# Four edits to a transformer block on one core: order of early work, row staging, statistics, slot products

## The chip, the cores and the metric

The kernel runs on one core of a Trainium2 chip. A core has five engines that run their own instruction queues and meet only at semaphores: PE (matmul), DVE (vector), ACT (scalar activations), POOL (GpSimd) and SP (here: issuing DMAs). The metric is the device time of one execution in microseconds, the median of 3 runs.

## What is computed

Two layers of cross-attention, each followed by a routed feed-forward, on x of 4 batches x 512 tokens x 256, with a context of 4 x 1024 x 256:

```python
def _L0_xattn_ref(encoder_hc, decoder_hq, w_sim, b_sim, W_qv, b_qv):
    Sim = (encoder_hc @ w1)[:, :, None] + (decoder_hq @ w2)[:, None, :] + jnp.einsum('bid,bjd->bij', encoder_hc * w3, decoder_hq) + b_sim[0]
    A = jax.nn.softmax(Sim, axis=2)
    hq_hat = jnp.einsum('bij,bjd->bid', A, decoder_hq)
    Batt = jax.nn.softmax(jnp.max(Sim, axis=2), axis=1)
    hc_bar = jnp.einsum('bi,bid->bd', Batt, encoder_hc)[:, None, :]
    feats = jnp.concatenate([encoder_hc, hq_hat, encoder_hc * hq_hat, encoder_hc * hc_hat], axis=-1)
    return feats @ W_qv + b_qv
...
x = x + _L0_xattn_ref(_layernorm(x, axis=-1), ctx_1024, ...)
x = x + _L0_ffn_ref(_layernorm(x, axis=-1), ...)     # top 2 of 12, 8 experts of 512 (silu), 4 pass x through
x = x + _L1_xattn_ref(_layernorm(x, axis=-1), ctx_1024, mask, ...)   # 4 heads of 64
x = x + _L1_ffn_ref(_layernorm(x, axis=-1), ...)     # top 2 of 8 experts of 1024 (gelu)
return x
```

## The kernel before

Tokens lie in 16 tiles of 128 rows, four to a batch; x stays in SBUF (`m.x`). Products that need the precision of fp32 are made from a high and a low part: ACT writes the high part (`..._hi`), DVE or POOL subtracts it for the low part (`..._lo`), and PE multiplies three pairs. The order on every engine is written out by hand; an instruction waits only at its queue's head, so all that stands behind it waits too.

Attention 0 (lines 124 to 715) handles one 128-row tile of scores at a time: PE makes scores, DVE the row maximum, ACT the exponential, DVE the reciprocal, POOL scales the rows (`normal`), PE transposes them (`turn`), ACT and DVE split the transposed rows (`high_parts`, `low_parts`), and PE multiplies them with the context (`values`). `make_u` and `u_low` (lines 520 to 530) form the query operand u of a batch; `scores(1, 0)` on PE waits for `u_lo` of batch 1 and for six halves of split context, `raw_lo`, of which the sixth is DVE's `split_low(2, ct_hi[1], ct_lo[1], 1)` on line 604. At the end of each batch `add_projection` (line 563) adds the result to x and takes the four tiles' statistics (`batch_stats`).

Expert layer (lines 1504 to 2151, twice; tiles are named b_ in layer 0 and d_ in layer 1). A preamble normalises x from the statistics, transposes it in 8 pairs of tiles, makes the routing logits, and from them on DVE a chain of small operations that ends in a table of slots. PE's `low_parts` (line 1851) and ACT's `low_out` (line 1761) form the low parts of the experts in `PE_LOW`, in chunks through two PSUM banks (2 an expert in layer 0, 4 in layer 1), while DVE writes `in_blk`, `val` and 32 one-hot tiles `in_lane`; 32 slot products (line 1883) follow. POOL then gathers token rows (line 1715) and PE starts 39 blocks: transpose (line 1892), up (1903), down (1913, 1916). `warm(n)` are products whose result nobody reads. The block of engine programs that holds one stage ends when all its engines have ended; only then is the next begun.

Attention 1 (lines 718 to 1501), in one block with expert layer 0: for batch 0 the rows the experts wrote (`ybuf`) are added by DVE at once. For batches 1 to 3, `add_experts` on POOL (line 882) scales rows by their gate weight and adds them to x by a DMA that accumulates; SP loads these rows (`load_y`, line 822). The tiles of `y_of` that hold them are, for batch 1, `prob[2]` and `prob[3]`, which the softmax of unit 1 writes too. So DVE waits on line 1420 for both of batch 1's accumulating DMAs (`sum_d1`) ahead of `both_maxima(0, 1)`. `summed(b)` takes the statistics of a batch whose sum is complete.

## Time and profile before

| what | us |
| --- | --- |
| median of 3 runs | 996.9 (996.88 to 997.63) |
| the profiled execution, its own time | 997.82 |
| its span, first to last instruction | 996.0 |
| PE busy | 895.6 (90%) |
| DVE busy | 622.6 (63%) |
| ACT busy | 519.4 (52%) |
| POOL busy | 436.4 (44%) |

The profile records each instruction with start, duration, source line, tiles and what released its engine. PE is busy in nearly all of the two expert loops; the stretches in which it is not are those that the change touches. Times below are us from the span's start.

### The profile page before, as it was taken

How to read it: one execution, taken by the hardware profiler on the slowest of the kernel's cores; microseconds unless marked ns; L12 is line 12 of the kernel's file. 1: busy time of each engine (PE TensorE's matmuls, PEld its weight loads, DVE VectorE, ACT ScalarE, POOL GpSimd, SP SyncE). 2: the span in 40 equal slices, each digit the busy share in tenths (PEclk: the TensorE clock that was granted, in tenths of full speed). 3: DMA queues.
4: the chain of work that ended last, by engine and by line, in shares of the span. 5: the costliest groups of instructions: out<-in, count | busy, mean ns of one | idle time of the engine just before them, and what ended most of it. 6: DMA issues, size and time to landing. Idle time of an engine off the chain costs nothing. (4 is left out here: it accounts for less than half of the span.)

```text
span 996.0 us, 19702 instructions
## 1 busy us (share of the span) xinstructions
PE 895.6 (90%) x6208; PEld 791.6 (79%) x6209; DVE 622.6 (63%) x1394; ACT 519.4 (52%) x1111; POOL 436.4 (44%) x374
## 2 busy tenths in 40 slices
PE   5899999868999998679899999987789999999995
PEld 4788989646899986468787787876379999999995
DVE  7875452485566676578778787774864455444552
ACT  5644140352344453487686686665655555555552
POOL 2374341004566672746264263220065556655542
PEclk9999999878999999699999999999889999999998
DMA  9621000365667738601020000006957676666762
GB/s 302 234 86 43 1 1 1 105 219 184 232 224 232 259 136 230 132 22 43 1 65 22 17 28 1 27 1 200 347 183 200 205 210 189 196 201 206 207 185 37
DMA packets 69652, 134.75 MB, mean 135 GB/s; under 512 B 8112, under 2 KB 51760, under 8 KB 64464
## 3 DMA queue, kind: packets, MB, share of 16 engines
q1 hardware_dynamic: 56240, 110.27, 32.7%
q0 software_dynamic: 13344, 23.63, 10.8%
q8 instruction: 37, 0.61, 0.2%
q14 instruction: 31, 0.25, 0.1%
HBM read 109.08 MB, written 21.64 MB: 131 GB/s over the span
## 5 line engine op out<-in xcount | busy, mean ns | idle before, releaser
L1807 ACT ACTIVATE x<-d_hps,b 128x128 f32<-128x128 f32 x312 | 89.0, 368 | 115.3 <-PE d_hps L1903 115.1
L1903 PEld LDWEIGHTS d_hps<-d_xg_t,d_xw 128*128 128x128 f32 x1248 | 146.5, 193 | 2.4 <-DVE d_xg_t L2084 0.9
L1903 PE MATMUL d_hps<-d_xg_t,d_xw 128*128 128x128 f32 x1248 | 146.9, 277 | 0.5 <-DVE d_xg_t L2084 0.5
L879 POOL TENSOR_SCALAR c_prob<-c_prob,c_rinv 128x1024 f32<-128x1024 f32 x64 | 72.0, 1143 | 130.3 <-DVE c_rinv L1338 129.9
L1913 PE MATMUL d_yps<-d_w,d_hid_hi 128*128 x312 | 115.2, 402 | 0.0
L1732 POOL DMA_INDIRECT out_x<-d_y,d_take_slot x39 | 63.1, 1619 | 97.0 <-DVE d_y L2121 87.8
L2084 DVE TENSOR_SCALAR d_xg_t<-d_take,ln_w,ln_b 128x128 f32<-128x128 f32 x78 | 28.4, 406 | 92.7 <-PE d_take L1892 82.9
L1345 DVE TENSOR_TENSOR c_pt_lo<-c_tp,c_pt_hi 128x512 fp32r<-128x512 f32 x128 | 82.3, 682 | 6.2 <-ACT c_pt_hi L1167 5.8
L1167 ACT ACTIVATE c_pt_hi<-c_tp 128x512 fp32r<-128x512 f32 x128 | 69.9, 597 | 25.8 <-PE c_tp L977 25.2
L977 PE MATMUL c_tp<-const,c_prob 128*128 128x128 f32 x512 | 71.7, 284 | 12.7 <-DVE c_pt_lo L1345 10.7
L1331 DVE CUSTOM_DVE_ANT_0 c_prob<-c_sc,c_minf 128x1024 f32<-128x1024 f32 x64 | 75.6, 1217 | 9.7 <-PE c_sc L964 9.7
L1916 PE MATMUL d_yps<-d_w,d_hid_lo 128*128 x312 | 81.2, 281 | 0.0
L1903 PEld LDWEIGHTS b_hps<-b_xg_t,b_w 128*128 128x128 f32 x624 | 77.8, 197 | 4.2 <-issue 2.6
L1903 PE MATMUL b_hps<-b_xg_t,b_w 128*128 128x128 f32 x624 | 78.3, 280 | 2.3 <-issue 2.3
L977 PEld LDWEIGHTS c_tp<-const,c_prob 128*128 128x128 f32 x512 | 60.0, 145 | 22.9 <-issue 16.3
L1715 POOL DMA_INDIRECT d_xg<-rows,d_take_slot x39 | 44.7, 1146 | 69.5 <-DVE d_take_slot L2052 57.9
L1160 ACT ACTIVATE c_prob<-c_prob,c_nmax 128x1024 f32<-128x1024 f32 x64 | 73.2, 1153 | 2.8 <-DVE c_nmax L1331 2.7
L1715 POOL DMA_INDIRECT b_xg<-rows,b_take_slot x39 | 44.3, 1137 | 63.0 <-DVE b_take_slot L2052 51.4
L1804 ACT ACTIVATE b_hid<-b_hps 128x256 f32<-128x256 f32 x78 | 29.4, 377 | 77.5 <-PE b_hps L1903 66.3
L1913 PEld LDWEIGHTS d_yps<-d_w,d_hid_hi 128*128 128x128 f32 x312 | 58.6, 188 | 9.7
L2093 DVE TENSOR_TENSOR d_hid_lo<-x,d_hid_hi 128x512 fp32r<-128x512 f32 x78 | 54.2, 696 | 12.5 <-ACT d_hid_hi L1813 12.0
L1913 PE MATMUL b_yps<-b_w,b_hid_hi 128*128 x156 | 61.4, 417 | 0.0
(376 smaller groups left out, 2195.6 us busy)
## 6 DMA issues: line engine op xcount, KB each, us to landing
d_xw<-in_w SPq DMA_DIRECT2D x39, 1024.0 KB
b_w<-in_w SPq DMA_DIRECT2D x47, 512.0 KB, 7.6
d_w<-in_w SPq DMA_DIRECT2D x8, 1024.0 KB, 12.0
a_raw<-in_ctx_t SPq DMA_DIRECT2D x8, 512.0 KB, 6.8
a_raw<-in_ctx SPq DMA_DIRECT2D x8, 512.0 KB, 4.6
ybuf<-a_zero SPq DMA_DIRECT2D x2, 2048.0 KB
k_stage<-in_ctx_t SPq DMA_DIRECT2D x12, 256.0 KB, 3.1
rows<-b_xn_all SPq DMA_DIRECT2D x1, 2048.0 KB, 12.9
```

What stands on the lines that cost most here:

```text
L879: nc.gpsimd.tensor_scalar(prob[w][:], prob[w][:], rinv[:, w:w + 1], 1.0, ALU.mult, ALU.mult).then_inc(s["prob_ready"], 1)
L977: mm = nc.tensor.transpose(tp[half][:, j * P:(j + 1) * P], prob[(2 * u + side) % 4][:, at:at + P], ident)
L1160: nc.scalar.activation(prob[w][:], prob[w][:], ACT.Exp, scale=-1.0, bias=nmax[:, w:w + 1], accum_out=rsum[:, w:w + 1]).then_inc(s["exp_don ...
L1167: nc.scalar.activation(pt_hi[side][:, half * 4:half * 4 + 4, t * P:(t + 1) * P], tp[half][:].rearrange("p (j i) -> p j i", i=P), ACT.Copy) ...
L1331: nc.vector.tensor_tensor_reduce(out=prob[w][:], in0=sc[side][:], in1=minf[:, t, :], scale=-1.0, scalar=BIG, op0=ALU.add, op1=ALU.min, acc ...
L1345: nc.vector.tensor_tensor(pt_lo[side][:, js, t * P:(t + 1) * P], tp[half][:].rearrange("p (j i) -> p j i", i=P), pt_hi[side][:, js, t * P: ...
L1715: nc.gpsimd.indirect_dma_start(out=xg[n % GATHERS][:], out_offset=None, in_=dram["rows"], in_offset=bass.IndirectOffsetOnAxis(ap=take_slot ...
L1732: nc.gpsimd.indirect_dma_start(out=dram["out"], out_offset=at, in_=y[n % LANES][:], in_offset=None, compute_op=ALU.add).then_inc(scattered ...
L1807: op = nc.scalar.activation(hid[q][:, h * FH + c, :], src[:, c, :], ACT.Gelu_apprx_tanh, bias=b1[:, ds(e, 1), h * FH + c])
L1903: mm = nc.tensor.matmul(hps[j % 2][h][:, c * P:(c + 1) * P], w1[j % WL][:, k, at:at + P], xg_t[j % 2][:, k, :], start=(k == 0), stop=(k == ...
L1913: both = lambda: nc.tensor.matmul(out[:].rearrange("p s d -> p (s d)"), hid_hi[j % 2][:, c, :], w2[:, ds(e, 1), c, :, :].rearrange("p a s ...
L1916: low = lambda: nc.tensor.matmul(out[:, 0, :], hid_lo[j % 2][:, c, :], w2[:, ds(e, 1), c, 0, :].rearrange("p a d -> p (a d)"), start=False ...
```

## The change

1. In attention 0, DVE's `make_u(1)` moves ahead of `split_low(1, ...)`, and `u_low(1)` ahead of `split_low(2, ...)`.
2. In attention 1 the rows of batches 2 and 3 are loaded by quarter-tile DMAs into unused parts of `pt_lo` and `pt_hi`; all scaled rows go to `scaled`, two tiles outside the softmax's; SP loads `y2` whole ahead of `y3`; POOL does only batch 1 ahead of the softmax, batch 2 behind units 0 and 1, batch 3 behind units 1 and 2. DVE waits for the scaling (`sum_p`) in place of the DMAs, and `summed(1)` moves behind the maxima.
3. The statistics of batches 0 to 2 are finished inside each attention (ACT's `root`, DVE's `variance` and inverse), those of batch 3 in the next expert preamble, behind the normalising of the tiles 4 to 11; the preamble's first normalising waits for nothing. `warm(12)` becomes `warm(5)`.
4. `val[..., 0]` and the last 8 `in_lane` tiles (Abs, then Relu) move from DVE to ACT, behind the first two experts' `low_out`. In layer 1 the third expert of `PE_LOW` is done behind the slot products, its `low_out` behind ACT's `high` of experts 5 to 7; `HIGH_AT` is (3, 5).

```diff
-                nc.scalar.activation(m.spare1[:], m.const[:, C_EPS:C_EPS + 1], ACT.Sqrt)
+                root(BUT_LAST, 20)
...
+                    if p < B - 1:
+                        dve.wait_ge(s["x_ready"], 2 * p + 2)
+                        batch_stats(nc, m, p).then_inc(s["bn_done"], 1)
...
                 maximum(0, 3)
+                make_u(1)
                 dve.wait_ge(s["raw_lo"], KD + 1)
                 split_low(1, cn_hi[0], cn_lo[0], 1)
                 low_parts(1)
                 invert(0, 3)
+                u_low(1)
                 dve.wait_ge(s["raw_lo"], 2 * KD + 1)
                 split_low(2, ct_hi[1], ct_lo[1], 1)
-                make_u(1)
-                u_low(1)
...
+                    if not now:
+                        dve.wait_ge(s["bn_done"], T + B - 1)
+                        variance(nc, m, dve, s["stat"], BUT_LAST, 14)
+                        inverse_std(nc, m, dve, s["stat"], s["sqrt_done"], BUT_LAST, 14, 3)
...
-        y_of = [(xn[:], tiles(ctx_t[:])), (tiles(prob[2][:]), tiles(prob[3][:])), (tiles(att_rows), xn[:]),
-                [halves(tile[:, :, (TB - 1) * P:TB * P].bitcast(F32)) for tile in pt_hi]]
+        y_of = [(xn[:], tiles(ctx_t[:])), (tiles(prob[2][:]), tiles(prob[3][:])),
+                *[[halves(tile[:, :, (TB - 1) * P:TB * P].bitcast(F32)) for tile in pair] for pair in (pt_lo, pt_hi)]]
+        scaled = (tiles(att_rows), xn[:])
...
-                if b == B - 1:
+                if b > 1:
                     for h in range(KD):
...
-            load_y(2, 0)
+            for k in range(2):
+                load_y(2, k)
...
-            sp.wait_ge(s["xn_tp"], KD)
-            load_y(2, 1)
...
+                if b > 1:
+                    pool.wait_ge(s[f"sum_d{b - 1}"], 16 * k + 16)
+                elif k:
+                    pool.wait_ge(s["xn_tp"], KD)
...
             for k in range(2):
                 add_experts(1, k)
-                add_experts(2, k)
...
                     if b == 0 and u < 2:
-                        add_experts(3, u)
+                        add_experts(2, u)
+                    if b == 0 and 1 <= u <= 2:
+                        add_experts(3, u - 1)
...
-                else:
+
+                if b == 0:
+                    dve.wait_ge(s["sum_p"], 2 * TB)
+                both_maxima(b, 1)
+                if b == 0:
                     summed(1)
-
-                if b == 0:
-                    dve.wait_ge(s["sum_d1"], 32)
-                both_maxima(b, 1)
...
+            variance(nc, m, dve, s["stat"], cols(0, B - 1), 15)
             for n in (6, 7):
                 head_sum(B - 1, n)
+            late_scale(0, B - 1, 15, 3)
             add_projection(B - 1, 0, xb)
             add_projection(B - 1, 1, tp[1])
-            new_stats(B - 1)
...
-    HIGH_AT = (1, 3, 5, 7) if first else (3, 7)
+    HIGH_AT = (1, 3, 5, 7) if first else (3, 5)
+    LOW_LATE = PE_LOW[len(PE_LOW):] if first else PE_LOW[-1:]
+    LANES_ACT = 8
...
+                if i == 2:
+                    act.wait_ge(s["stat"], 7)
+                    nc.scalar.activation(m.std[:, LAST], m.var[:, LAST], ACT.Sqrt, ...)
...
+            def value_parts():
+                act.wait_ge(s["blk_ready"], 1)
+                nc.scalar.activation(val[:, :, 0, :], in_blk[:], ACT.Copy, scale=...).then_inc(s["val0_ready"], 1)
+                for n in range(2 * T - LANES_ACT, 2 * T):
+                    op = nc.scalar.activation(off[:, n - tail.start, :], c16(C_ROW, P), ACT.Abs, scale=-1.0, bias=...)
+                op.then_inc(s["off_ready"], 1)
+                act.wait_ge(s["off_ready"], 1)
+                nc.scalar.activation(in_lane[:, tail, :], off, ACT.Relu, ...).then_inc(s["lane_act"], 1)
+
+            for e in PE_LOW[:2]:
                 low_out(e)
+            value_parts()
             for e in DVE_LAST:
                 high(e)
+            for e in LOW_LATE:
+                low_out(e)
...
-            warm(12, rank)
+            warm(5, rank)
...
+            for e in LOW_LATE:
+                low_parts(e)
             warm(8, rank)
...
-            stats_chain(nc, m, dve, s["stat"], s["sqrt_done"])
-            for t in range(ACT_TILES, T):
+            for t in range(ACT_TILES, T - TB):
+                normalise(nc, m, xn_all[:, t, :], t).then_inc(s["xn_dve"], 1)
+            batch_stats(nc, m, B - 1).then_inc(s["stat"], 1)
+            dve.wait_ge(s["stat"], 1)
+            stats_chain(nc, m, dve, s["stat"], s["sqrt_done"], LAST, 1)
+            for t in range(T - TB, T):
                 normalise(nc, m, xn_all[:, t, :], t).then_inc(s["xn_dve"], 1)
```

## Rows read from the trace of the kernel before

**Rows 1.** windows view: busy us (x instructions) per engine, granted clock, DMA share, GB/s.

```profile
205.00:219.00 14.00, 8.14 (x21) 4.14 (x20) 12.39 (x36) 4.17 (x6) 0.00 (x0) 0.51 0.42 150
```

**Rows 2.** timeline view, PE at 38 us: start, duration, instruction, [idle before <-releaser].

```profile
38.36 0.79 PE L242 MATMUL a_sc<-a_ct_hi,a_u_hi 128*128 128x512 f32 x1 [3.37 <-DVE a_u_lo L529]
```

**Rows 3.** timeline view, DVE, 30 to 40 us.

```profile
32.71 1.23 DVE L534 TENSOR_TENSOR a_ct_lo<-a_raw,a_ct_hi 128x1024 fp32r<-128x1024 f32 x1 [1.22 <-POOL a_ct_lo L672]
...
33.85 0.81 DVE L523 TENSOR_SCALAR a_u_t<-a_ex,a_wsim 128x512 f32<-128x512 f32 x1
...
35.36 2.95 DVE L529 TENSOR_TENSOR a_u_lo<-a_u_t,a_u_hi 128x512 fp32r<-128x512 f32 x2 [0.70 <-ACT a_u_hi L426]
```

**Rows 4.** timeline view, POOL, 30 to 38 us.

```profile
30.31 2.37 POOL L672 TENSOR_TENSOR a_ct_lo<-a_raw,a_ct_hi 128x1024 fp32r<-128x1024 f32 x1 [1.58 <-DVE a_cn_lo L534]
...
32.66 2.19 POOL L679 TENSOR_SCALAR a_prob<-a_prob,a_rinv 128x1024 f32<-128x1024 f32 x1
...
34.81 2.35 POOL L685 TENSOR_TENSOR x<-x,a_bqv 128x1024 f32<-128x1024 f32 x1
```

**Rows 5.** timeline view, DVE, then POOL, 367 to 372 us.

```profile
368.80 2.15 DVE L2093 TENSOR_TENSOR b_hid_lo<-b_hid,b_hid_hi 128x256 fp32r<-128x256 f32 x2 [0.26 <-ACT b_hid_hi L1813]
...
369.63 1.04 POOL L807 TENSOR_SCALAR c_minf<-c_minf 128x1024 bf16<-128x1024 bf16 x1 [0.19 <-POOL c_minf L804]
```

**Rows 6.** timeline view, end of attention 0 and expert layer 0: DVE, PE, ACT.

```profile
186.62 1.40 DVE L119 BATCH_NORM_STATS2 bn<-x 128x6 f32<-128x256 f32 x4
...
221.04 5.28 DVE L2041 TENSOR_SCALAR b_in_lane<-c,b_lane 128x128 bf16<-128x128 bf16 x32
...
201.41 0.96 PE L1847 MATMUL b_lps<-b_gw,b_xn_t 128*128 128x12 f32 x8
...
202.85 0.96 PE L1847 MATMUL b_lps<-b_gw,b_xn_t 128*128 128x12 f32 x8
...
204.85 1.28 PE L1847 MATMUL b_lps<-b_gw,b_xn_t 128*128 128x12 f32 x8
...
191.39 2.08 ACT L1770 ACTIVATE b_xn_all<-x,nmr,rstd 128x256 f32<-128x256 f32 x4 [0.53 <-DVE nmr L1955]
...
217.44 0.60 ACT L1764 ACTIVATE b_w<-b_low 128x512 fp32r<-128x512 f32 x1 [1.54 <-PE b_low L1858]
...
220.47 0.60 ACT L1764 ACTIVATE b_w<-b_low 128x512 fp32r<-128x512 f32 x1 [0.49 <-PE b_low L1858]
```

**Rows 7.** timeline view, attention 1, batch 0: POOL, then DVE.

```profile
391.28 0.99 POOL L897 DMA_DIRECT2D x<-c_prob  x1 [0.31 <-POOL c_prob L892]
...
416.84 0.87 POOL L897 DMA_DIRECT2D x<-k_rows  x1 [0.30 <-POOL k_rows L892]
...
406.50 1.41 DVE L119 BATCH_NORM_STATS2 bn<-x 128x6 f32<-128x256 f32 x4 [5.22 <-DMA x<-c_prob]
...
428.06 1.39 DVE L119 BATCH_NORM_STATS2 bn<-x 128x6 f32<-128x256 f32 x4
```

**Rows 8.** DMA issues of 385 to 430 us: KB each, median us from issue to landing.

```profile
x<-k_rows POOLq DMA_DIRECT2D x2, 512.0 KB, 4.7
```

**Rows 9.** timeline view, attention 1's end and expert layer 1: SP, DVE, ACT, PE.

```profile
678.67 0.37 SPq L819 DMA_DIRECT2D out_x<-x  x1
...
696.73 2.29 DVE L1961 TENSOR_TENSOR d_w<-d_w 128x2048 fp32r<-128x2048 f32 x1 [3.46 <-ACT d_w L1759]
...
728.95 6.68 DVE L1961 TENSOR_TENSOR d_w<-d_w 128x2048 fp32r<-128x2048 f32 x3
...
719.69 5.50 ACT L1759 ACTIVATE d_w<-d_w 128x2048 fp32r<-128x2048 f32 x3
...
719.00 1.32 PE L1883 MATMUL d_slots<-d_val,d_in_lane 128*128 128x80 bf16 x32
...
720.16 1.71 PE L1827 MATMUL d_rank<-c 128*128 128x456 bf16 x8
...
726.42 1.11 PE L1892 MATMUL d_take<-const,d_xg 128*128 128x128 f32 x4 [4.55 <-DMA d_xg<-rows,d_take_slot]
```

More of the change, by code:

```diff
@@ L1283, in scalar @@
                 head_part(B - 1, n)
-            nc.scalar.activation(m.spare1[:], m.const[:, C_EPS:C_EPS + 1], ACT.Sqrt)
+            root(0, B - 1, 21)
         def vector(dve):
@@ L1363, in new_stats @@
                 dve.wait_ge(s["x_ready"], b * 2 + 2)
-                batch_stats(nc, m, b)
+                batch_stats(nc, m, b).then_inc(s["x_bn"], 1)
             def both_maxima(b, u):
@@ L1586, in experts @@
         in_lane = sr("in_lane", [P, 2 * T, P], BF16)
+        off = xt[:, 0:LANES_ACT * P // 2].bitcast(BF16).rearrange("p (n j) -> p n j", j=P)
         rowf = sr("rowf", [P, NBX])
@@ L1783, in scalar @@
             nc.scalar.activation(e2[:], dlog[:], ACT.Exp).then_inc(s["exp_ready"], 1)
-            for e in PE_LOW:
+            def value_parts():
+                act.wait_ge(s["blk_ready"], 1)
+                nc.scalar.activation(val[:, :, 0, :], in_blk[:], ACT.Copy, scale=m.const[:, C_TOKEN:C_TOKEN + 1]
+                                     ).then_inc(s["val0_ready"], 1)
+                tail = slice(2 * T - LANES_ACT, 2 * T)
+                for n in range(2 * T - LANES_ACT, 2 * T):
+                    op = nc.scalar.activation(off[:, n - tail.start, :], c16(C_ROW, P), ACT.Abs, scale=-1.0,
+                                              bias=lane[:].rearrange("p k t -> p (k t)")[:, n:n + 1])
+                op.then_inc(s["off_ready"], 1)
+                act.wait_ge(s["off_ready"], 1)
+                nc.scalar.activation(in_lane[:, tail, :], off, ACT.Relu, scale=-1.0,
+                                     bias=m.const[:, C_ONES:C_ONES + 1]).then_inc(s["lane_act"], 1)
+            for e in PE_LOW[:2]:
                 low_out(e)
+            value_parts()
             for e in DVE_LAST:
                 high(e)
+            for e in LOW_LATE:
+                low_out(e)
             nc.scalar.activation(m.spare1[:], m.const[:, C_EPS:C_EPS + 1], ACT.Silu if first else ACT.Gelu_apprx_tanh)
@@ L1885, in tensor @@
             mm.then_inc(s["slots_done"], 1)
+            for e in LOW_LATE:
+                low_parts(e)
             warm(8, rank)
@@ L2035, in vector @@
             by_b = lambda a: a.unsqueeze(2).broadcast_to([P, 2 * T, NBX])
-            after(V.tensor_tensor(in_blk[:], c16(C_BLK, NBX).unsqueeze(1).broadcast_to([P, 2 * T, NBX]),
-                                  by_b(blk[:].rearrange("p k t -> p (k t)")), ALU.is_equal))
-            V.tensor_scalar(val[:, :, 0, :], in_blk[:], m.const[:, C_TOKEN:C_TOKEN + 1], None, ALU.mult).then_inc(s["val_ready"], 1)
+            V.tensor_tensor(in_blk[:], c16(C_BLK, NBX).unsqueeze(1).broadcast_to([P, 2 * T, NBX]),
+                            by_b(blk[:].rearrange("p k t -> p (k t)")), ALU.is_equal).then_inc(s["blk_ready"], 1)
+            dve.wait_ge(s["blk_ready"], 1)
             V.tensor_tensor(val[:, :, 1, :], in_blk[:], by_b(c16(C_TILE, 2 * T)), ALU.mult).then_inc(s["val_ready"], 1)
-            for n in range(2 * T):
+            for n in range(2 * T - LANES_ACT):
                 op = V.tensor_scalar(in_lane[:, n, :], c16(C_ROW, P), lane[:].rearrange("p k t -> p (k t)")[:, n:n + 1], None, ALU.is_equal)
```

37 lines of the change are left out of this document (19 added, 18 removed).

## The prediction

> **What bounds the kernel now.** The table of busy time comes first: PE works for 90% of the span, and the windows show that in both expert loops it has no gap worth naming. A shift that reaches the first block of such a stretch is carried to the end in full; one that ends in a wait is lost. So the second view is the windows around the stretches where PE is not full. One of them is [rows 1]: at 205 to 219 us PE works 8.14 of 14.00 us at a granted clock of 0.51, the level of 1.2 GHz, while DVE works 12.39. The third view is the timeline in the four places that the diff touches: 30 to 40 us (unit A below), 187 to 230 (B), 391 to 430 (C), 678 to 737 (D). In each the question is what the instruction that restarts PE waits for, and what comes second. The profiled execution took 997.82 us, its span 996.0, and the median is 996.9. I make the sum against 997.82 and take 0.9 off for the median.
>
> **A, u of batch 1 ahead: +0.7 us (from -2.0 to +2.2).** PE stands still for 3.37 us until `a_u_lo` is there and makes scores(1, 0) at 38.36 [rows 2]. That product needs the sixth half of split context too, which is DVE's `split_low(2, ...)`, so both orders must do the same DVE work ahead of it; only the meeting with POOL changes. In the trace POOL's split runs from 30.31 for 2.37 us [rows 4] and DVE's from 32.71 with 1.22 us of waiting on it [rows 3]. `make_u` costs 0.81 [rows 3]. Ahead of `split_low(1, ...)` it delays DVE's split, and with it POOL's, which waited for DVE's half [rows 4], from 30.31 to 31.1. Then DVE and POOL want SBUF together. How they share it shows in three places: the two `u_low` take 2.95 us [rows 3] for some 1.3 of work while POOL's `normal` takes 2.19 [rows 4]; two subtractions of 256 columns take 2.15 us with a POOL operation of 1.04 between them [rows 5]. So an operation of one comes between two of the other. I string them in the new order: 31.1, POOL's split 2.4, first `u_low` 0.6, `normal` 1.1, second `u_low` 0.6, POOL's `add_bias` 2.3 (it took 2.35, [rows 4]), DVE's split 1.1. That ends at 39.2; 0.2 of hand-offs overlaps, so scores(1, 0) starts at 39.0 against 38.36. If DVE's split gets ahead of `add_bias`, it starts at 36.9, which is -1.4. The high end adds one more stretch at the low clock.
>
> **B, expert layer 0's start: -2.6 us (from -4.0 to -1.0).** The `batch_stats` at 186.62, 1.40 us [rows 6], leave the end of attention 0, and the block ends by that much earlier. In the preamble ACT's first four tiles of xn start at 191.39, after 0.53 of idle behind the statistics [rows 6]; with these made earlier they follow the block's start, 189.1 now. That is 2.3. So the pairs of tiles on PE, which begin as ACT's four tiles end (191.39 + 2.08), begin 2.3 + 1.4 = 3.7 us earlier. Against this stands the clock: `warm(12)` becomes `warm(5)`, and the pairs may begin colder. A pair took 1.44 us (202.85 less 201.41) at the high level; eight logit products took 0.96 in it and 1.28 where the level dropped [rows 6]. So a cold pair takes between 1.92 (the same ratio) and 2.88 (twice all of it), and I take 2.3. I take off 1.3 for one and a half such pairs, 0.86 each; the logits are 2.4 earlier.
> Then the slots. DVE loses `val[..., 0]` (0.47) and eight of 32 `in_lane` (5.28 / 32 = 0.165 each, 1.3; [rows 6]). The work that takes their place on ACT is in no row. I bound it by ACT's other operations: 0.60 for 512 columns [rows 6] and 5.50 / 3 = 1.83 for 2048 [rows 9] give, as estimates by a straight line, 1.21 for the Copy of 1280 columns, 0.29 for each Abs of 128 (2.3 for eight) and 1.01 for the Relu; with hand-offs 4.75. Its least is 3.0, if 128 columns cost no more than 0.1. It stands behind the two experts' `low_out`, whose last ends at 220.47 + 0.60. The four chunks come at PE's pace: 1.54 + 0.60 = 2.14 apart at the low clock, 0.49 + 0.60 = 1.09 at the high one [rows 6]. With the logits 2.4 earlier the last chunk ends near 219.5, value parts near 224.3, while DVE would have its lanes by 222.3: ACT ends last, and slots are done at 224.5 against 227.1. This is the -2.6. ACT had been idle here, so nothing else hides behind it.
> The Trainium skill (ScalarE: Activation LUTs, section on table sets as the hidden batching unit) says that cheap functions, relu, copy, identity and abs, are in every set. By that the two new functions load no table; no row of before shows either. Were a load needed after all, the same page (What ACT_TABLE_LOAD costs) puts it near 2.7 us with its drain, and the sum of B would be about 0.
>
> **C, staging of rows in attention 1: -1.9 us (from -4 to 0).** DVE waits 5.22 us on the accumulating DMA before the statistics at 406.50 [rows 7]; the maxima of unit 1 stand behind this, then its exponentials and PE's transposes. The new wait is on POOL's scaling, which ends by about 400 with the issue that now stands at 391.28 [rows 7]. So the maxima come up to 4.9 us earlier (5.22 less a hand-off). What is late next: batch 3's second accumulating DMA. It was issued at 416.84 [rows 7], and such a transfer lands 4.7 us after its issue [rows 8]. POOL now does batches 2 and 3 between units, each behind the DMA before it, and batch 2's second pair, which was over by the issue before, now stands in between (four scalings and an issue, 2.1 + 0.9, twice, less the time by which all of it starts earlier, and one landing waited for): I put the issue at 421.5 and the landing at 426.2. `summed(3)` ran at 428.06 without idle [rows 7]; moved up by 4.9 it would be at 423.2 and must then wait until 426.2. Gain 1.9. SP issues eight quarter-tile loads in place of four, but these end well before they are needed. If the statistics don't wait, -4.1 stays (4.9 less 0.8 for PE at the low clock); if the maxima were only early and PE's own work paces the units, nothing is gained. I take the value between because [rows 7] show no slack at 428.06.
>
> **D, expert layer 1's start: +1.6 us (from 0 to +4).** The block of attention 1 ends with the new statistics gone, but SP's output DMA at 678.67 (0.37) [rows 9] still has to be issued: 1.0 earlier, no more. DVE's `weights_low(1)` waited 3.46 for ACT's high part at 696.73 and took 2.29 [rows 9], and the copy of the logits stood behind it; with `high` behind pair 5 and not 7 the copy waits for the pairs alone, 2.5 to 3 earlier. DVE's lanes and value parts on ACT go as in B, and the slot products, 1.32 us at 719.00 [rows 9], are done near 717.7, 2.6 earlier. But now the third expert's low parts stand behind them. ACT does three `high` first, 5.50 us [rows 9]: 717.2 + 5.5 = 722.7. Then `low_out` of chunk 0 (0.60) frees the bank for PE's chunk 2, and the second one likewise; two chunks of PE at 1.1 to 2.1 each follow, and `warm(8)` of 1.71 [rows 9] (3.1 cold) stands behind. PE's first take was bound by the gather, 4.55 us of waiting, at 726.42 [rows 9]. The gathers start 2.6 earlier and their rows land near 723.8, but PE comes to it only between 727.2 and 730.6; I take 728.0, +1.6, the lower half, since PE works there without a gap until then. Behind it DVE's `weights_low` of three, 6.68 us from 728.95 [rows 9], is no later than before and covers part of it, which is why the low end is 0.
>
> **Sum:** 0.7 - 2.6 - 1.9 + 1.6 = -2.2; 997.82 - 2.2 = 995.6, and for the median 994.7.
>
> **The rivals.**
> Shared port turns the other way (A -1.4 instead of +0.7): 994.7 - 2.1 = 992.6. For it: DVE is ready first when POOL's `normal` ends. Against: POOL has no other work between the two, and DVE has a second `u_low` [rows 3, 4].
> Staging's second wait doesn't come (C -4.1): 992.5. It does so if POOL issues before 418.5. Against: `normal` of units 1 and 2 stands between.
> The change doesn't do what it says in the preambles: value parts are late on ACT, the low chunks pace them, and B gives 1.0 or less: 996.3. For it: the idle of 1.54 and 0.49 before `low_out` [rows 6] says that PE's chunks set ACT's time there, and these depend on the clock, not on when ACT starts.
> Slower: TensorE stays at 1.2 GHz through the pairs. The mechanism has one place: fewer warm products, so no high level before the first pair. Six of eight pairs at some 2.3 instead of 1.44 us cost 5.0 in layer 0. In layer 1, where the twelve products were not needed up to the first pair, two such pairs cost 1.8. It decides at the last logits: if these come later than in before, the sum turns. Together 994.7 + 6.8 = 1001.5 in full, about 999 if only the first layer. For it: the windows of the trace show 0.51 wherever PE was slack, as at 205 us [rows 1]. Against: in [rows 6] the level held through the pairs with their own work alone, and fell only at their end (1.28).
> Here the Trainium skill (TensorE: Matmul & The Clock Gate, Part 1: The HAM clock gate) speaks against the change: "the default state is throttled, and activity releases the throttle". By that, products taken away ahead of the pairs put the rise later; the trace agrees as far as that the low level follows slack.
>
> **How the numbers follow.** Forecast 0.40; port the other way 0.13; no second wait 0.10; preambles give nothing 0.17; low clock 0.20. The range goes from 990.8 (both favourable rivals together give 990.4) to 999.5, which leaves out the clock case at its full price. The forecast's own range is 992.7 to 996.7. About 0.2%, or 2 us, is what a measurement of this kernel can tell from no change. The forecast lies 2.2 below, so about half of its own spread of 2 us each way is within the bound. Faster: 0.24 of the forecast, 0.13 of the port's case, 0.08 of no second wait: 0.45. Same: 0.14 of the forecast, 0.02 of no second wait, 0.15 of the idle preambles, 0.02 of the low clock: 0.33. Slower: 0.02 of the forecast, 0.02 of the preambles, 0.18 of the low clock: 0.22.
>
> **Signs to look for.** A: POOL's `add_bias` ahead of DVE's `split_low(2, ...)`, and scores(1, 0) at 39.0. B: the pairs 1.44 us apart from the second on, as in [rows 6]; slots finished 2.6 earlier than before. C: no idle on the accumulating DMA before the maxima of unit 1, but idle of about 3 us in front of the statistics of batch 3. D: PE idle ahead of its last two low chunks, and the first take starting well after its gather has landed. What would make it wrong: slots that are no earlier (B), a clock of 0.5 up to the logits, or experts' loops that no longer start as one PE-bound stretch, so that the shift isn't carried.

## The result

Twenty runs of each kernel: 997.73 us (median) before, 990.75 after, 7.0 less. The ratio is 0.9925 with a 95% interval of 0.991 to 0.994, which is 7.5 us (6 to 9). The forecast, 994.7, was 2.2 less, with a range of 990.8 to 999.5: the direction was right, the gain three times too small, and the measured time lies just below the range.

The profiled execution of the changed kernel took 988.45 us (span 986.4), 9.4 less than that of before. That is 2.4 more than the medians tell, so single stages of one pair of traces can't be taken at their word. I therefore traced both kernels a second time, and give stage lengths of both traces each. A runs up to the start of the last projection product of attention 0; B from there to the end of the slot products of layer 0; the loop's start from there to the start of the 98th up product of layer 0; C from the first maxima of attention 1 to those of batch 1's unit 4; D from the end of the last product of attention 1 to the start of the first down product of layer 1.

| stage | before | before, again | after | after, again | difference of means | forecast |
| --- | --- | --- | --- | --- | --- | --- |
| A | 185.5 | 184.7 | 182.9 | 184.5 | -1.4 | +0.7 |
| B | 41.6 | 40.1 | 36.5 | 37.1 | -4.1 | -2.6 |
| loop's start | 30.8 | 31.9 | 28.0 | 31.1 | -1.8 | 0 |
| C | 103.0 | 102.8 | 101.9 | 101.9 | -1.0 | -1.9 |
| D | 58.9 | 61.4 | 61.0 | 60.6 | +0.6 | +1.6 |
| all the rest | 576.3 | 576.2 | 576.1 | 576.4 | 0 | 0 |

The sum of the differences is -7.6, near the 7.0 of the medians and the 7.5 of the ratio. Two traces a side are few: before's two differ by 2.5 in D and by 1.5 in B, after's by 3.1 at the loop's start.

### The profile page after: what moved, and what is told of

It is laid out like the page before. It is cut to its first block and busy times, and to the rows that moved or that the text cites. A ratio compares the mean times of both kernels' runs of the same rounds, so it can differ in the third digit from the quotient of the medians.

```text
span 986.4 us, 19692 instructions
## 1 busy us (share of the span) xinstructions
PE 891.9 (90%) x6194; PEld 788.2 (80%) x6195; DVE 624.0 (63%) x1390; ACT 527.9 (54%) x1131; POOL 431.4 (44%) x374
## 5 line engine op out<-in xcount | busy, mean ns | idle before, releaser
L2126 DVE TENSOR_SCALAR d_xg_t<-d_take,ln_w,ln_b 128x128 f32<-128x128 f32 x78 | 28.4, 406 | 93.0 <-PE d_take L1931 92.8
L1177 ACT ACTIVATE c_pt_hi<-c_tp 128x512 fp32r<-128x512 f32 x128 | 69.8, 597 | 22.1 <-PE c_tp L987 21.7
L1731 POOL DMA_INDIRECT d_xg<-rows,d_take_slot x39 | 38.3, 981 | 69.2 <-DVE d_take_slot L2094 57.7
```

Of the source, the lines that this page charges most:

```text
L1177: nc.scalar.activation(pt_hi[side][:, half * 4:half * 4 + 4, t * P:(t + 1) * P], tp[half][:].rearrange("p (j i) -> p j i", i=P), ACT.Copy) ...
L1731: nc.gpsimd.indirect_dma_start(out=xg[n % GATHERS][:], out_offset=None, in_=dram["rows"], in_offset=bass.IndirectOffsetOnAxis(ap=take_slot ...
```

## The profile after, stage by stage

A. DVE, then POOL, then PE, timeline from 33 to 38 us (start, duration, instruction, idle before and its releaser):

```profile
33.11 2.42 DVE L530 TENSOR_TENSOR a_u_lo<-a_u_t,a_u_hi 128x512 fp32r<-128x512 f32 x2
35.45 2.06 DVE L535 TENSOR_TENSOR a_ct_lo<-a_raw,a_ct_hi 128x1024 fp32r<-128x1024 f32 x1
...
32.01 2.38 POOL L680 TENSOR_TENSOR a_ct_lo<-a_raw,a_ct_hi 128x1024 fp32r<-128x1024 f32 x1 [2.49 <-DVE a_cn_lo L535]
34.35 2.09 POOL L687 TENSOR_SCALAR a_prob<-a_prob,a_rinv 128x1024 f32<-128x1024 f32 x1
36.40 3.37 POOL L693 TENSOR_TENSOR x<-x,a_bqv 128x1024 f32<-128x1024 f32 x1
...
38.03 0.40 PE L243 MATMUL a_sc<-a_ct_hi,a_u_hi 128*128 128x512 f32 x1
```

DVE issues its split at 35.45, while POOL's `normal` still runs. It is through at 37.51, 1.1 us behind the end of `normal` (36.44), and POOL's `add_bias`, which I had put ahead of it, is the one that waits: 3.37 us in place of 2.35 [rows 4], with its end (39.77) 2.3 behind the split's. In the same way the two `u_low` end 1.1 behind the end of POOL's split (35.53 against 34.39). From the start of POOL's split DVE needs 5.50 us for all its operands here, and 8.0 in before (30.31 to 38.31, [rows 3, 4]). PE has no idle before 38.03 any more, against 3.37 [rows 2]. The start of scores(1, 0) itself says little, since all that lies ahead of it moves from one execution to the next (38.0 and 39.2 in the two traces of after, 38.4 and 39.0 in those of before). It can be counted from the last DVE operation ahead of the edit, the maximum of unit 3; here that operation in before, then in after:

```profile
27.87 1.22 DVE L540 TENSOR_REDUCE a_nmax<-a_sc 128x1 f32<-128x1024 f32 x1 [0.46 <-PE a_sc L242]
...
28.67 1.23 DVE L541 TENSOR_REDUCE a_nmax<-a_sc 128x1 f32<-128x1024 f32 x1 [0.47 <-PE a_sc L243]
```

From it to scores(1, 0) it is 10.5 us in each of the four traces with the old order, and 8.9 to 9.4 in each of the twelve with the new one.

B. PE at the end of attention 0 and in the preamble, then ACT, DVE and PE at the slots:

```profile
185.10 1.12 PE L1860 MATMUL b_rank<-c 128*128 128x456 bf16 x5 [1.83 <-PEq L2216]
186.36 0.66 PE L1872 MATMUL b_tpx<-const,b_xn_all 128*128 128x128 f32 x4
...
213.21 0.60 ACT L1780 ACTIVATE b_w<-b_low 128x512 fp32r<-128x512 f32 x1 [0.49 <-PE b_low L1891]
213.70 1.35 ACT L1803 ACTIVATE b_val<-b_in_blk,const 128x1280 bf16<-128x1280 bf16 x1
214.95 2.43 ACT L1807 ACTIVATE b_xn_t<-c,b_lane 128x128 bf16<-128x128 bf16 x8
217.42 1.15 ACT L1811 ACTIVATE b_in_lane<-b_xn_t,const 128x1024 bf16<-128x1024 bf16 x1
...
213.67 3.99 DVE L2083 TENSOR_SCALAR b_in_lane<-c,b_lane 128x128 bf16<-128x128 bf16 x24
...
218.62 0.71 PE L1920 MATMUL b_slots<-b_val,b_in_lane 128*128 128x80 bf16 x8 [0.45 <-ACT b_in_lane L1811]
```

The five warm products take 0.22 us each: the high level. ACT's value parts take 4.87 us (213.70 to 218.57; 4.75 was the estimate), load no table, and end 0.9 behind DVE's 24 lanes, where DVE alone would have needed 1.3 + 0.5 more. The last `low_out` ends 14.55 us behind the copy of the logits (213.81 against 199.26), and 14.90 in before (221.07 against 206.17).

C. POOL's last accumulating DMA and DVE in batch 0 of attention 1:

```profile
392.37 1.23 DVE L1341 CUSTOM_DVE_ANT_0 c_prob<-c_sc,c_minf 128x1024 f32<-128x1024 f32 x1 [1.69 <-PE c_sc L974]
...
416.01 1.41 DVE L119 BATCH_NORM_STATS2 bn<-x 128x6 f32<-128x256 f32 x4 [2.87 <-DMA x<-k_rows]
...
411.49 0.87 POOL L906 DMA_DIRECT2D x<-k_rows  x1 [1.10 <-DMA x<-c_att_t]
```

The maxima of unit 1 no longer wait for a DMA but for PE; the wait has gone to the statistics of batch 3, 2.87 us, and answers to the 5.22 and to the missing idle of [rows 7].

D. ACT, DVE and PE in the preamble of layer 1:

```profile
702.67 1.35 ACT L1803 ACTIVATE d_val<-d_in_blk,const 128x1280 bf16<-128x1280 bf16 x1
703.92 2.43 ACT L1807 ACTIVATE d_xn_t<-c,d_lane 128x128 bf16<-128x128 bf16 x8
706.39 1.15 ACT L1811 ACTIVATE d_in_lane<-d_xn_t,const 128x1024 bf16<-128x1024 bf16 x1
...
697.96 3.99 DVE L2083 TENSOR_SCALAR d_in_lane<-c,d_lane 128x128 bf16<-128x128 bf16 x24
...
704.12 1.02 PE L1920 MATMUL d_slots<-d_val,d_in_lane 128*128 128x80 bf16 x24 [1.98 <-issue]
707.59 0.72 PE L1920 MATMUL d_slots<-d_val,d_in_lane 128*128 128x80 bf16 x8 [2.44 <-ACT d_in_lane L1811]
...
713.56 1.12 PE L1889 MATMUL d_low<-d_w,const 128*128 x2 [0.44 <-issue]
715.84 1.71 PE L1860 MATMUL d_rank<-c 128*128 128x456 bf16 x8
717.39 0.60 PE L1931 MATMUL d_take<-const,d_xg 128*128 128x128 f32 x4
```

DVE's lanes are done at 701.95, but the slots' last products wait for ACT until 707.54: ACT reached its value parts only behind eight `low_out`. The take follows PE's low parts and `warm(8)` without any wait on the gather, where in before it waited 4.55 for it [rows 9].

## Experiments

**Both kernels again.**

> The kernel before, unchanged, a second trace of it. It tells which low-clock stretches belong to the kernel and which to the single execution. If the stretch at half clock at the start of expert layer 0 (12 warm products in 4.72 us at 189.11) and the one behind the wait for a block's weights at 252.67 are the kernel's own, both come again within 1 us of their place, and the first transpose stands again 4.5 us behind the first warm product. If they are chance, at least one is gone, and the span is 2 to 3 us shorter. The dip at 171 to 177 us (granted clock 0.72) I hold for chance: even odds that it comes again.

> The changed kernel, unchanged, a second trace of it. If its stage gains are its own: scores(1, 0) within 0.5 us of 38.0, warm(5) at the high level (1.1 us), slots of layer 0 within 1.5 us of 219.3, idle of 2 to 3.5 us at the statistics of batch 3 on the accumulating DMA, slots of layer 1 12 us and the first take 17 to 18 us behind the last ... of the logits' copy at 684.8 less 1. If the gain of 9.6 us between the two profiled executions was partly chance (the medians say 7.0), the span is 987 to 991 here.

Measured: spans 997.1 and 991.6, so before's second was no shorter and after's just above the 987 to 991 expected. Of before's low stretches, the one behind the standstill at 252 us came again, and so did the dip at 171 us. Ahead of layer 0 the twelve warm products were only partly low the second time (3.6 us from the first to the first transpose, not 4.5), and the whole start of layer 0 was 1.5 us shorter. Of after, the stage gains came again except at the loop's start (28.0, then 31.1), where a block of the low level stood in the second trace alone, and the wait at the statistics of batch 3 (3.34). Two marks missed what was expected: scores(1, 0) came at 39.21 and the slots of layer 0 were done at 221.6, since attention 0 took 1.6 us longer than in the first trace. So of the 9.6 us between the first two traces some 2 were chance; the second two are 5.5 apart.

**A undone.**

```diff
-                make_u(1)
                 dve.wait_ge(s["raw_lo"], KD + 1)
...
-                u_low(1)
                 dve.wait_ge(s["raw_lo"], 2 * KD + 1)
                 split_low(2, ct_hi[1], ct_lo[1], 1)
+                make_u(1)
+                u_low(1)
```

> The changed kernel with make_u(1) and u_low(1) back in their old place. Theory 1 (the reordering only swaps which of PE's two waits is long; two traces of each kernel put scores(1, 0) at 38.0 and 39.2 with it, 38.4 and 39.0 without): scores(1, 0) between 38 and 39.2, total 0 +- 1. Theory 2 (the port's turns make the old order cheaper, as forecast): scores(1, 0) at 38.4 and total -0.7. Theory 3 (the edit is worth what attention 0 is shorter by in the two pairs of traces): end of attention 0 1.4 us later, total +1.4.

Measured: 992.73 us, ratio to before 0.9951 (0.9931 to 0.9971). Stage A took 185.4 us. With the three traces of other kernels in the old order (185.5, 184.7, 185.2) the mean is 185.2; the twelve traces in the new order have 182.9 to 184.7, mean 183.7. The edit gains 1.4 us, theory 3, and the 10.5 against 8.9 to 9.4 us from the maximum to scores(1, 0) tell the same. The times tell 2.6 (0.9951 against 0.9925), with intervals that overlap. DVE and POOL in this kernel:

```profile
32.91 2.19 POOL L687 TENSOR_SCALAR a_prob<-a_prob,a_rinv 128x1024 f32<-128x1024 f32 x1
35.07 2.34 POOL L693 TENSOR_TENSOR x<-x,a_bqv 128x1024 f32<-128x1024 f32 x1
...
35.61 2.95 DVE L530 TENSOR_TENSOR a_u_lo<-a_u_t,a_u_hi 128x512 fp32r<-128x512 f32 x2 [0.70 <-ACT a_u_hi L427]
```

With POOL's 2.34 us running, the two `u_low` take 2.95 again; moved ahead they take 2.42. That PE starts scores(1, 0) at 38.62, only 0.6 later than in after, is not the whole of it: the products behind are low here (0.79 for the first) and high in after (0.40). In before's second trace they were high too, and its stage A is the shortest of the old order.

**The clock in the preambles: gap and number of warm products.** Four kernels around the changed one and before:

```diff
# warm12; before_warm5 is the reverse, in before
-            warm(5, rank)
+            warm(12, rank)
# stats_back (stats12: both)
-                    if p < B - 1:
-                        dve.wait_ge(s["x_ready"], 2 * p + 2)
-                        batch_stats(nc, m, p).then_inc(s["bn_done"], 1)
+                    dve.wait_ge(s["x_ready"], 2 * p + 2)
+                    batch_stats(nc, m, p).then_inc(s["bn_done"], 1)
...
             add_projection(B - 1, 1, tp[1])
+            new_stats(B - 1)
```

> The changed kernel with 12 warm products instead of 5 at the start of both expert layers. Theory 1 (the shorter gap ahead of the preamble keeps TensorE at 2.4 GHz, the number of warm products decides nothing): the 12 run at the high level in 2.4 us, end about 1.2 us after the tiles are ready, the pairs run 1.44 us apart as before; logits and all behind 1.0 to 1.3 us later in layer 0 and 0 to 0.6 in layer 1; total +1 to +2 us. Theory 2 (fewer products cost clock, which other gains hide): pairs or the low chunks run faster than with 5, logits no later than now, total -1 to 0.

> The changed kernel with the statistics of batch 3 computed once more at the end of both attentions, where they stood in the kernel before (the result is overwritten later); 1.40 us of DVE work that the block's end waits for. Theory 1 (the gap decides the clock): PE's gap in front of layer 0 grows from 2.9 back to 4.3 us less nothing, its first warm products fall to the low level (0.39 us each), and logits come 1.4 + 1 to 3 = 2.4 to 4.4 us later. Theory 2 (the gap costs its own length only): logits 1.4 us later in layer 0, 0.9 in layer 1, pairs 1.44 apart; total +2.3.

> The kernel before with 5 warm products instead of 12 in both preambles, nothing else. Theory 1 (the gap of 3.25 us in front of the preamble drops the clock, and twelve products were what brought it back): in layer 0 the pairs stay at the low level, 2.3 to 2.9 us apart instead of 1.44, logits 5 to 9 us later, total +5 to +9 in most runs. Theory 2 (the number decides nothing): PE is free 2.7 us earlier and waits for the tiles, first transpose 1.5 us earlier, pairs 1.44 apart, total -1.5 to 0.

> The changed kernel with the statistics of batch 3 computed once more at the end of both attentions (the result is overwritten later), and 12 warm products instead of 5: the fourth corner beside the kernels with the statistics back and 5 products, with 12 products alone, and the changed kernel. Theory 1 (gap and number act together: behind the long gap of 3.3 us the clock is low, and twelve products bring it back before the pairs, five do not): the 12 run low (0.39 each, 4.7 us) and the pairs come 1.44 apart, not 2.75; logits of layer 0 about 16 to 17 us behind the first warm product, as in the kernel before (17.1), not 23.7; no time above 1000. Theory 2 (the number decides nothing behind a long gap either): pairs 2.75 apart in layer 0 and times spread from 992 to 1010 as with 5.

| kernel | PE idle ahead of layer 0 | warm products | first warm product to logits, layer 0 | time, us | ratio to before |
| --- | --- | --- | --- | --- | --- |
| before | 3.25 | 12 | 17.1, 15.5 | 997.73 | 1 |
| before, 5 products | 3.26 | 5 | 25.5 | 1012.61 | 1.0148 (1.0098 to 1.0197) |
| after | 1.83 | 5 | 14.2, 14.8 | 990.75 | 0.9925 (0.991 to 0.994) |
| after, 12 products | 1.83 | 12 | 14.4 | 991.58 | 0.9944 (0.9918 to 0.9971) |
| after, statistics back | 3.27 | 5 | 23.7 | 998.58 | 0.999 (0.9962 to 1.0019) |
| after, statistics back, 12 products | 3.27 | 12 | 14.2 | 994.64 | 0.9982 (0.9964 to 1.0) |

Each ratio is to runs of before made beside the kernel's own; before's median went from 995.6 to 998.3 us between such sets, so times of different rows are best compared by their ratios.

PE's timeline in the kernel with the statistics back, in before with 5 products (layer 0, then layer 1), and with statistics back and 12 products, one fence each:

```profile
187.19 2.06 PE L1860 MATMUL b_rank<-c 128*128 128x456 bf16 x5 [3.27 <-PEq L2216]
189.04 2.77 PE L1872 MATMUL b_tpx<-const,b_xn_all 128*128 128x128 f32 x12
191.60 1.72 PE L1880 MATMUL b_lps<-b_gw,b_xn_t 128*128 128x12 f32 x8
...
193.50 1.06 PE L1872 MATMUL b_tpx<-const,b_xn_all 128*128 128x128 f32 x4
```

```profile
188.86 2.06 PE L1827 MATMUL b_rank<-c 128*128 128x456 bf16 x5 [3.26 <-PEq L2174]
195.03 1.72 PE L1847 MATMUL b_lps<-b_gw,b_xn_t 128*128 128x12 f32 x8
...
687.18 2.06 PE L1827 MATMUL d_rank<-c 128*128 128x456 bf16 x5 [3.66 <-PEq L2182]
693.35 1.71 PE L1847 MATMUL d_lps<-d_gw,d_xn_t 128*128 128x8 f32 x8
```

```profile
186.60 2.47 PE L1860 MATMUL b_rank<-c 128*128 128x456 bf16 x12 [3.27 <-PEq L2216]
188.91 1.59 PE L1872 MATMUL b_tpx<-const,b_xn_all 128*128 128x128 f32 x12
190.33 0.96 PE L1880 MATMUL b_lps<-b_gw,b_xn_t 128*128 128x12 f32 x8
```

The windows view of the second kernel, one line for each preamble, has 0.50 granted from the first to the last pair:

```profile
188.00:214.00 26.00, 23.78 (x108) 21.19 (x109) 10.04 (x26) 14.00 (x20) 0.00 (x0) 0.50 0.80 258
686.00:712.00 26.00, 23.45 (x106) 20.86 (x107) 9.65 (x24) 13.00 (x17) 0.00 (x0) 0.50 0.97 304
```

So theory 1 holds where it says that gap and number act together. Behind 3.3 us of idle ahead of layer 0 five products left all eight pairs at 1.2 GHz in both traces (pairs 2.75 apart, logits 9 us late; 2.4 to 4.4 was expected with the statistics back, and for before with 5 products a total of +5 to +9 where 14.8 came), and in before with 5 products in layer 1 too; twelve never did, whether they ran low themselves (4.72 us in before) or high (2.47 in stats12; here the clock had not fallen, which theory 1 had not expected). Behind 1.83 us, ahead of layer 0, five were enough in each of the nine traces that have them.

Layer 1 is less clear-cut. First the changed kernel, then the one with the statistics back:

```profile
668.93 2.06 PE L1860 MATMUL d_rank<-c 128*128 128x456 bf16 x5 [2.79 <-PEq L2224]
```

```profile
686.53 1.12 PE L1860 MATMUL d_rank<-c 128*128 128x456 bf16 x5 [3.71 <-PEq L2224]
```

Behind 2.79 us of idle the five ran low in four of those nine traces (2.0 to 2.06 us), both of the changed kernel among them, and the pairs behind them still came 1.44 us apart: the level was back by the first pair's logits. And behind 3.71 us, the longest idle ahead of a preamble in any trace, the five ran high with the statistics back. So a long gap makes the loss possible and not certain, and three cases of it (both layers of before with 5, layer 0 with the statistics back) are all that the traces have.

The effect is not in each execution: with the statistics back and 5 products the ten times run from 991.7 to 1010.1, with 12 from 992.6 to 997.2. Twelve in the changed kernel put the transposes 2.3 us behind the first product instead of 1.3, but the logits no later (14.4 against 14.2 and 14.8), and cost nothing that the times can tell. The Trainium skill (TensorE: Matmul & The Clock Gate, Part 1: The HAM clock gate) has it that "activity releases the throttle"; the traces agree for the twelve low ones of before and the five low ones of layer 1 behind 2.79 us, behind which the pairs ran high; behind five in the two windows above the level stayed as it was, to the end of the pairs.

**Value parts on DVE, by layer.** One flag sends the Copy and the last eight lanes back to DVE:

```diff
# vals1_dve; vals0_dve has "not first"
+    ON_ACT = first
-    LANES_ACT = 8
+    LANES_ACT = 8 if ON_ACT else 0
...
-            value_parts()
+            if ON_ACT:
+                value_parts()
...
             dve.wait_ge(s["blk_ready"], 1)
+            if not ON_ACT:
+                V.tensor_scalar(val[:, :, 0, :], in_blk[:], m.const[:, C_TOKEN:C_TOKEN + 1], None, ALU.mult).then_inc(s["val_ready"], 1)
```

> The changed kernel, but in layer 1 alone DVE makes all 32 lane tiles and the first half of val again (ACT's Copy, eight Abs and Relu are gone there). Theory 1 (ACT's value parts, 4.87 us behind its eighth low_out, set the slots and, with three highs behind them, the third expert's low parts): in the changed kernel lanes 1 to 24 were done 5.0 us before the last value part; 1.9 us of DVE work comes back, so slots are done 3.5 to 4.2 us earlier, ACT's highs start 4.8 earlier, the first take is 4.3 to 5.0 earlier, and total -4 to -5. Theory 2 (the first take waits for the third expert's weights or gathers anyway): slots as above, but the first take moves by less than 1.5, total -1.5 to 0.

> The changed kernel with the value parts of layer 0 on DVE and those of layer 1 left on ACT. In the changed kernel ACT's Relu ends 0.9 us behind DVE's 24 lanes in layer 0, and DVE would need 1.9 for what ACT does. Theory 1 (ACT gains where its low_out is done early, with two experts, and loses where there are three): slots of layer 0 0.9 to 1.1 us later measured from the logits, total +0.5 to +1.2. Theory 2 (ACT is the wrong place in both layers): slots of layer 0 earlier, total below 0.

Measured: with layer 1's on DVE 986.45 us, ratio 0.9886 (0.9848 to 0.9924), 4 us less than the changed kernel, though the two intervals still overlap. From the logits to the end of the slots it took 19.4 us in place of 22.1 and 23.5; the take came 8.87 behind the slots (9.08). Stage D fell from 61.0 and 60.6 to 57.4. Theory 1, if by less than it had: the first take came 2.0 and 3.7 us earlier, counted from attention 1's end, and not 4.3 to 5.0. With layer 0's on DVE: 991.39, 0.9951 (0.9926 to 0.9975), logits to slots 20.9 us, as in before, in place of 20.1. So by the traces ACT gains 0.8 in layer 0 and loses 3.4 in layer 1, and the same edit has both signs; that the times of layer 0's kernel agree (0.9951 against 0.9925) is no proof, as their intervals overlap.

**Low parts of the third expert ahead of ACT's highs**, with the value parts of layer 1 on DVE:

```diff
-            for e in DVE_LAST:
-                high(e)
             for e in LOW_LATE:
                 low_out(e)
+            for e in DVE_LAST:
+                high(e)
```

> The kernel with the value parts of layer 1 on DVE, and besides ACT's low_out of the third expert ahead of its highs of experts 5 to 7 (PE's order as in the changed kernel). Theory 1 (the first take waits for PE's third low parts, and these for ACT's highs): the first take comes 4.9 us behind the slots, as the gather allows, plus at most 1.5, instead of 8.87; highs end 4.4 later than there but still ahead of DVE's weights_low; total -2 to -3.5 against the kernel with value parts of layer 1 on DVE alone, so 983 to 984.5. Theory 2 (DVE's weights_low of three, 6.68 us, start with the highs): the first take is earlier, the first down product is not; total 0 to -1.

Measured: 987.63 us, 0.9875 (0.9836 to 0.9914), no different from 0.9886. PE was through with its low parts and warm products at 713.70, but:

```profile
708.96 1.48 SPq L1673 DMA_DIRECT2D d_xw<-in_w  x2
...
709.06 1.09 POOL L1732 DMA_INDIRECT d_xg<-rows,d_take_slot  x1 [52.47 <-DMA rows<-d_xw]
...
716.10 0.67 PE L1934 MATMUL d_take<-const,d_xg 128*128 128x128 f32 x2 [2.40 <-DMA d_xg<-rows,d_take_slot]
```

The first gather lands 7.0 us after its issue, where in before it took 4.2 (722.20 to 726.4), and 2.9 in before's second trace. It was issued within 0.1 us of the two transfers of the first block's weights (2 MB), and POOL had to wait for the write of `rows`; in before these weights had been issued at 717.60, 4.6 us ahead of it. Neither theory is quite it: the take is held by the gather. With the value parts of layer 1 on DVE alone PE had been through at 715.52 and took at 716.09, 7.0 behind its gather's issue at 709.10. So the take stands as long behind the gather's issue in both, and PE, through 1.8 us earlier here, only waited longer. What makes the gather slow is not shown: the 2 MB were not tried by themselves, and the write of `rows` was late as well.

**C undone, and the later wait moved.**

```diff
# noC: y_of, load_y, add_experts and their order as in before, and
-                if b == 0:
-                    dve.wait_ge(s["sum_p"], 2 * TB)
-                both_maxima(b, 1)
-                if b == 0:
+                else:
                     summed(1)
+                if b == 0:
+                    dve.wait_ge(s["sum_d1"], 32)
+                both_maxima(b, 1)
# later_sum3
                 if b == 0:
-                    summed(3)
-                    dve.wait_ge(s["x_bn"], B)
-                    variance(nc, m, dve, s["stat"], cols(1, B - 1), 7)
+                    dve.wait_ge(s["sum_d3"], 16)
                 head_sum(b, 0)
...
                 both_maxima(b, 4)
                 if b == 0:
+                    summed(3)
+                    dve.wait_ge(s["x_bn"], B)
+                    variance(nc, m, dve, s["stat"], cols(1, B - 1), 7)
```

> The changed kernel with the old staging of the expert rows in attention 1 (rows of batch 1 scaled in place in softmax tiles, old order of loads, DVE's wait for both of batch 1's sums ahead of the maxima of unit 1). Theory 1 (the gain is what remains of it behind the later wait for batch 3's sum, 2.87 us): DVE idles about 5 us ahead of the statistics of batch 1 and not at all ahead of batch 3's, unit 4's maxima 1.5 to 2.2 later, total +1 to +2. Theory 2 (the whole wait counts): total +4 to +5. Theory 3 (given back by the end of batch 0, PE's own work paces): total 0 to +0.5.

> The changed kernel with the statistics of batch 3 and the variance in attention 1 moved behind the maxima of unit 4, so that DVE waits for the last accumulating sum (2.87 us of idle in the changed kernel) only after it has released unit 4; head_sum(0) waits for the first of batch 3's two transfers instead. Theory 1 (the wait gives back 1.4 to 2 us of what the staging gained): maxima of units 4 about 2 us earlier, total -1 to -2. Theory 2 (the last sum is needed by the next chain, the normalising of batches 1 to 3, as soon): the idle moves behind the maxima, unit 5 is late by as much, total 0 +- 0.7.

Measured: 993.28 us for C undone, 0.9951 (0.993 to 0.9972); 988.33 for the later wait, 0.9895 (0.9844 to 0.9945). From the first maxima to those of unit 4 it takes 34.7 to 35.1 us in three traces of the old staging in before, 35.05 with C undone, 32.9 and 33.05 in the changed kernel: -1.9 at this point. At unit 4 of batch 1 the same four are 101.9 to 103.0, 102.2, and 101.9 twice. Over all traces the four with the old staging have a mean of 102.5 there and the twelve with the new one 101.9, from 100.3 to 103.1. So more than half of the 1.9 is given back in between; the times can't tell 0.5 from 2. Moving the later wait brought the maxima of unit 4 4.6 us earlier (28.4), and at unit 5 nothing was left of it (41.3 us behind the first maxima, 40.9 in the changed kernel), C 101.9 again: theory 2. Its time, 2.4 us below the changed kernel's, comes from four runs and an interval 10 us wide. DVE there, then ACT:

```profile
416.83 1.23 DVE L1341 CUSTOM_DVE_ANT_0 c_prob<-c_sc,c_minf 128x1024 f32<-128x1024 f32 x1
...
419.12 1.40 DVE L119 BATCH_NORM_STATS2 bn<-x 128x6 f32<-128x256 f32 x4
...
423.29 1.29 DVE L1355 TENSOR_TENSOR c_pt_lo<-c_tp,c_pt_hi 128x512 fp32r<-128x512 f32 x2 [1.08 <-ACT c_pt_hi L1177]
...
421.43 0.30 ACT L1198 ACTIVATE std<-var,const 128x12 f32<-128x12 f32 x1 [4.17 <-DVE var L95]
...
425.06 1.15 ACT L1170 ACTIVATE c_prob<-c_prob,c_nmax 128x1024 f32<-128x1024 f32 x1
```

DVE has no wait for a DMA left and is 4.6 us ahead, and still the next units are no earlier. The wait has gone to ACT: its square root for batches 1 to 3 stands in its queue ahead of unit 4's exponential, and the edit left that order as it was. ACT stands still for 4.17 us until DVE's variance, now behind the maxima, is there (2.56 in the changed kernel), and the exponential of unit 4 comes 36.7 us behind the first maxima, where the changed kernel has 36.2. Moving ACT's root too was not tried.

**All together.**

> Both of the two kernels beside it together: value parts of layer 1 on DVE, low_out of the third expert first, statistics of batch 3 behind unit 4. If the gains are of separate places they add: ratio to the kernel before 0.9886 less 0.002 to 0.0035 less 0 to 0.002, some 982 to 985 us. If they share a bound, no better than the better of the two.

> The same with 12 warm products instead of 5 in both preambles. Theory 1 (with the short gap five are enough): +0.7 to +1.5 in the median. Theory 2 (in some executions five are too few, which is the tail of the changed kernel's times at 996 to 998): the median is the same and the highest time lower.

Measured: 986.40 us, 0.9881 (0.9845 to 0.9917), and with 12 warm products 990.02, 0.99 (0.9865 to 0.9935). The gains don't add: the first of them is no better than the value parts of layer 1 on DVE by themselves. That kernel, at 986.45, beats before by 1.1%, is 0.4% below the changed kernel by the ratios and 3.4 us by stage D, and is the smallest step to it.

## Why the forecast was wrong

- **A (forecast +0.7, measured -1.4).** The step that failed is the string of turns between DVE and POOL. Behind POOL's split I put `u_low`, `normal`, `u_low`, `add_bias` and then DVE's split, 5.7 us. In the trace the first `u_low` is issued while POOL's split still runs (33.11, 1.1 behind its start at 32.01), both `u_low` are over 1.1 behind its end, `normal` 0.9 later and DVE's split 1.1 later still: 3.1 us, with `add_bias` last. DVE issued its split at 35.45, a microsecond before POOL issued `add_bias` at 36.40, and it went first. That was a rival, at -1.4 for scores(1, 0) and a chance of 0.13: counted from the maximum of unit 3 it came 1.1 and 1.5 us earlier in the two traces of after, so the rival's mechanism and size were right and its chance too small.
- **B (forecast -2.6, measured -4.1).** Barrier (1.4) and statistics (2.2; 2.3 was forecast) came as priced. Two terms were mis-sized. Lanes and value parts gave 0.8, and my sum gave them 0.2: it put the last `low_out` near 219.5, where 221.07 less the 2.4 of the logits is 218.7. And of the 1.3 us that I took off for cold pairs 0.4 is left in the mean of the traces (logits 3.2 earlier and not 2.4, out of 3.6), because of a stretch that I had not seen: in before the twelve warm products themselves ran low (0.39 each, 4.72 us) and held the first transpose back to 193.62, while the tiles were ready. With the gap at 1.83 us nothing fell, and the five ran high. I counted fewer warm products as a loss, and not the shorter gap, which the same edit brings, as the gain that pays for it. The slower rival was true as a mechanism: with the gap left as it was, five products cost 14.8 us (0.0148 of 997.7, over both layers), more than twice my 6.8, as a pair takes 2.75 cold and not 2.3, and all eight in both layers were cold. That the level held in the changed kernel is owed to the shorter gap, which the prediction did not name; its own reason against this rival, that the pairs' work alone holds the level, is not what decided.
- **Loop's start (forecast 0, measured -1.8 in two pairs).** Here the forecast had no term. PE stands still ahead of the sixth block in both kernels (2.27 us in before, 0.98 in after; I take it for the weights, the profile names no releaser), and behind the longer standstill the next 16 up products took 3.36 us and not 2.0: low level. Over all traces the 98th up product comes 27.5 to 31.9 us behind the slots without order by kernel, so some of this is chance, and how much isn't settled.
- **C (forecast -1.9, measured -1.0 in the end).** The mechanism was as told to the tenth: no wait at unit 1, 2.87 us at the statistics of batch 3 (about 3 was forecast), -1.9 at unit 4. The step that failed is the one that carried it on: attention 1 is not bound by PE alone at that point (PE is busy for 84 of the 102 us up to unit 4 of batch 1, and ACT's square root waits for the same statistics), so a shift there isn't carried whole.
- **D (forecast +1.6, measured +0.6).** The copy of the logits came 3.0 us earlier, counted from attention 1's end. The slots gained nothing more: ACT's value parts end at 707.54, 3.7 behind where DVE alone would have its lanes (701.95 + 1.3 + 0.55). And the take stood 9.1 behind the slots where before had 4.9 and 6.1, as told. The sign is the forecast's, but before's two traces are 2.5 apart, so it is not sure. The largest single loss of the change lies here; with the value parts back on DVE stage D is 3.4 us shorter.

The direction of the whole was right: B and C came with the forecast's sign, and A, which was thought to cost, gained too. The size was missed by 2.1 us in A, where the turns came the other way, by 1.5 in B, by 1.8 at the loop's start, of which an unknown part is chance, and by 1.0 in D; C took 0.9 back.

## What to carry to other kernels

Price a shorter gap and the warm products behind it together: here five warm products were enough behind 1.83 and 2.79 us of idle, and behind 3.3 us or more they failed in three cases of four. Where two engines slow each other, string their operations by the time at which each is issued, and not one from either in turn: here both `u_low` went ahead of `normal`, and of `add_bias` and DVE's split the one issued first kept its place (the two `u_low` took 2.95 us behind `add_bias`, `add_bias` 3.37 behind DVE's split). And work that is moved to an idle engine must be looked at in every place where the same code runs: here it gained 0.8 us behind four chunks and lost 3.4 behind eight. And a wait that is moved on one engine must be moved on every engine whose queue holds it: ACT's square root took up what DVE had been freed of.

## What was not expected of the hardware

Behind the same idle the clock was low in one execution and high in another: in before, ahead of layer 1, 3.66 us were followed by twelve warm products in 2.47 us in the first trace and in 4.72 in the second. So one trace of a stage with such a gap is good to some 2 us and, with few warm products behind it, to 9. The low level held for 26 us through a whole preamble (granted clock 0.50), with PE shown busy for 23.8 of them. An indirect gather that took 4.2 and 2.9 us from issue to landing in before took 7.0 when issued together with two 1 MB transfers; whether by them is open.
